# Sixteen-row blocks by DMA for the base inverse of a gated delta-rule kernel, and a new order of the turn

## The reference

```python
xn = layernorm(x)
# attention: q, k, v = silu(conv4(xn @ W)); k *= 128 ** -0.5
# alpha, beta = sigmoid(xn @ Wa + ba), sigmoid(xn @ Wb + bb)
def step(S, inps):                      # one token; S is 128 x 128 for each batch and head
    qt, kt, vt, at, bt = inps
    err = S @ kt - vt
    S = at * S - bt * outer(err, kt)
    return S, S @ qt
S0 = zeros; o = scan(step, S0, tokens)
o = (o - mean(o)) * rsqrt(var(o) + 1e-5) * ln_w + ln_b
attn = (o * sigmoid(xn @ Wg)) @ Wo
# experts: 512 tokens, 16 experts, top 4, silu(gate) * up, down, weighted sum
out = x + attn + moe
```

## Time and profile before

| | us |
|---|---|
| median of three runs | 3923.6 |
| the profiled execution | 3925.09 |
| its span, first to last instruction | 3923.5 |
| PE busy | 3769.9 (96%) |
| DVE, ACT, POOL busy | 2704.0, 2204.4, 1281.8 |
| mean granted TensorE clock | 0.986 |
| `prepare` ends on PE | 476.1 |
| `heads`, first to last instruction on DVE and POOL | about 486 to 3549.4 |
| `project` ends | about 3918 |

### The profile page before, as it was taken

How to read it: one execution, slowest core, us unless ns; L and a number is a source line. 1 busy time by engine, 2 the same in 40 slices (tenths; PEclk the granted TensorE clock), 3 DMA queues, 4 the chain that set the end, 5 groups by cost and what they waited for, 6 DMA issues and landing times. The chain is left out here.

```text
span 3923.5 us, 119759 instructions
## 1 busy us (share of the span) xinstructions
PE 3769.9 (96%) x41088; PEld 3063.9 (78%) x41088; DVE 2704.0 (69%) x6942; ACT 2204.4 (56%) x6016; POOL 1281.8 (33%) x2594
## 2 busy tenths in 40 slices
PE   7999889999999999999999999999999999987999
PEld 5777668888888888888788888888888888866887
DVE  3444458878788777788777778777887878863222
ACT  3433356666666666666666666666666666652111
POOL 3434433333333333333333333333333333320000
PEclk9999989999999999999999999999999999988999
DMA  3343341111111211111321111111111211215443
GB/s 134 111 147 141 117 128 45 51 45 47 45 45 48 55 50 46 45 48 48 90 88 46 45 48 48 45 48 45 47 49 45 48 45 45 50 24 163 144 146 109
DMA packets 371786, 275.67 MB, mean 70 GB/s; under 512 B 153457, under 2 KB 284529, under 8 KB 369361
## 3 DMA queue, kind: packets, MB, share of 16 engines
q1 hardware_dynamic: 368848, 261.29, 23.5%
q0 software_dynamic: 2560, 8.39, 0.6%
HBM read 209.85 MB, written 59.77 MB: 69 GB/s over the span
## 5 line engine op out<-in xcount | busy, mean ns | idle before, releaser
L1084 DVE SCALAR_TENSOR_TENSOR conv<-bank,tap,conv 128x512 f32<-128x512 f32 x1152 | 857.6, 744 | 79.3 <-ACT conv L1233 56.4
L1295 PE MATMUL bank<-hx_hi,w_hi 128*128 128x512 f32 x2048 | 874.2, 427 | 35.2 <-POOL w_lo L913 24.0
L1295 PE MATMUL bank<-hx_hi,w_lo 128*128 128x512 f32 x2048 | 899.4, 439 | 0.0
L1295 PE MATMUL bank<-hx_lo,w_hi 128*128 128x512 f32 x2048 | 881.5, 430 | 0.0
L1295 PEld LDWEIGHTS bank<-hx_hi,w_hi 128*128 128x128 f32 x2048 | 391.3, 191 | 71.7 <-issue 49.0
L1295 PEld LDWEIGHTS bank<-hx_lo,w_hi 128*128 128x128 f32 x2048 | 389.0, 190 | 50.7
L931 POOL TENSOR_TENSOR prods<-Lb,Tc 128x28 f32<-128x28 f32 (+6 forms) x896 | 203.6, 227 | 683.6 <-ACT Lb L1219 621.2
L1295 PEld LDWEIGHTS bank<-hx_hi,w_lo 128*128 128x128 f32 x2048 | 389.9, 190 | 40.1
L965 POOL TENSOR_TENSOR oG<-oT,gT 128x512 f32<-128x512 f32 x128 | 163.7, 1279 | 721.7 <-ACT oT L1254 721.7
L1037 DVE SCALAR_TENSOR_TENSOR S<-S,gamma,bank 128x128 f32<-128x128 f32 x480 | 163.6, 341 | 203.9 <-PE bank L1376 191.7
L1207 ACT ACTIVATE Wc<-bank 128x128 f32<-128x128 f32 x512 | 141.4, 276 | 242.4 <-PE bank L1367 242.3
(11 more groups left out here) (156 smaller groups left out, 8836.3 us busy)
## 6 DMA issues: line engine op xcount, KB each, us to landing
gamma<-gamma_d SPq DMA_DIRECT2D x128, 258.0 KB, 3.4
alpha<-alpha_d SPq DMA_DIRECT2D x128, 256.0 KB, 3.1
oT_d<-oG SPq DMA_DIRECT2D x128, 256.0 KB, 2.4
o_raw<-oT_d SPq DMA_DIRECT2D x32, 1024.0 KB, 6.8
gu_raw<-in_gate_up SPq DMA_DIRECT2D x17, 1408.0 KB, 6.3
dn_raw<-in_down SPq DMA_DIRECT2D x17, 512.0 KB, 4.5
x_in<-in_x SPq DMA_DIRECT2D x8, 1024.0 KB, 9.3
w_raw<-in_Wk SPq DMA_DIRECT2D x32, 256.0 KB, 3.6
```

The costliest lines, as they stand in the source:

```text
L1084: dve.scalar_tensor_tensor(out=conv[i][:, to], in0=PJ[PJ_OF[(g + 3) % 4][i]][:], scalar=tap[:, i, j + 1:j + 2], in1=conv[i][:, to], op0=AL ...
L1295: last = pe.matmul(dst, a[:, i, k], b[:, k, cols], start=(j == 0), stop=(j == 3 * KC - 1))
```

## The change

The base block of the inverse becomes 16x16 (`SB` 16, `LEVELS` gone), one merge level falls away, and the blocks of L get to GpSimd by DMA:

- VectorE's diag, Lc and Lx, TensorE's product with `same` and ScalarE's copy to `Lb` are gone. SyncE's new `spread` stores the eight 16x16 diagonal blocks of LT to DRAM, one DMA for each block, and reads them back with four loads, each of which names two blocks 16 times over, so that each of 32 partitions gets its block's 256 values of 4 chunks (4096 B).
- GpSimd's substitution has 15 steps of two instructions instead of 7. It waits for all four loads. The pipeline is one group deeper: group g+4 is projected, and its solve begins in slot 35 and ends in slot 13 of the next turn.
- TensorE has two visits a turn (slots 20 and 1) with three groups in each: 16 matmuls of 32x32, 8 of 32x32 and 4 of 64x64. `MT32` and the columns of `w32` keep the two merges apart.
- Products with the zero state are left out: the first chunk of a head has no S by kT and no q_gamma by S, the last no k_rows by Wc and one transpose less.
- The slots of nearly all operations are new; kT and gT have 6 buffers, qT, vT, decay and TT three; the loop over the heads is unrolled by 3; weights are cut in other slots; ScalarE cuts the first weights before it waits for constants.

```diff
-SB = 8
+SB = 16
 TB = 32
-LEVELS = [8, 16]
+NB = P // SB
 STEPS = 38
-CHAIN = {0: 0, 5: 1, 8: 2, 11: 3, 13: 4, 17: 5, 20: 6, 24: 7, 26: 8, 29: 9, 32: 10, 34: 11}
+UNROLL = 3
+CHAIN = {0: 0, 6: 1, 8: 2, 13: 3, 15: 4, 17: 5, 19: 6, 21: 7, 23: 8, 29: 9, 31: 10, 35: 11}
-A_AT, KT_AT, VT_AT, ON_TURN_AT, L_AT, BASE_AT = 1, 2, 11, 18, 24, 30
-VISIT_AT = {9: 0, 15: 1, 28: 2, 34: 3}
-SOLVE_AT = {34: (0, 2), 36: (2, 4), 0: (4, 6), 2: (6, 7)}
+A_AT, KT_AT, VT_AT, ON_TURN_AT, L_AT = 5, 0, 9, 26, 18
+VISIT_AT = {20: 0, 1: 1}
+SOLVE_AT = {35: (0, 1), 0: (1, 4), 3: (4, 6), 6: (6, 9), 7: (9, 11), 9: (11, 14), 13: (14, 15)}
+T16P_AT, POW_AT, QG_AT, OG_AT = 19, 12, 21, 23
+AT_AT, K_AT, T16_AT, TN64_AT, DECAY_AT, LT_AT = 4, 3, 17, 16, 7, 18
+CUT_AT = {(3, 22): 0, (3, 27): 1, (3, 30): 2, (0, 2): 3}
...
+        base_d = nc.dram_tensor("base_d", (2, P // SB, SB, G, SB), F32, kind="Internal").ap()
...
-        diag = sb("diag", [P, G, TB])
-        Lc = sb("Lc", [P, G, SB])
-        Lx = sb("Lx", [P, G, SB, SB])
-        Lb = sb("Lb", [P, G, SB, SB])
+        Lb = sb("Lb", [P, SB, G, SB])
...
+            def spread(hh, g, d):
+                at = counter(hh, g)
+                place = base_d[(g + d) % 2]
+                for q in range(NB):
+                    rows = slice(q * SB, (q + 1) * SB)
+                    if q == 0:
+                        sp.wait_ge(lt_done, at(1, d + 1))
+                    if q == NB - 1:
+                        wait(sp, solve_done, at(SOLVE_PER, d))
+                    sp.dma_start(place[q], LT[rows, (g + d) % 4, :, rows], allow_slow_non_contiguous=True)\
+                      .then_inc(base_stored[q // 2], 16)
+                for i in range(NB // 2):
+                    sp.wait_ge(base_stored[i], at(32, d + 1))
+                    sp.dma_start(Lb[i * TB:(i + 1) * TB].rearrange("p i c t -> p (i c t)"),
+                                 place[2 * i:2 * i + 2].rearrange("b (o i) c t -> b o (i c t)", o=1)
+                                 .to_broadcast([2, SB, SB * G * SB])).then_inc(base_loaded[i], 16)
...
                             if i == 0:
-                                pool.wait_ge(lb_done, at(1, d + 1))
+                                for loaded in base_loaded:
+                                    pool.wait_ge(loaded, at(16, d + 1))
                             wait(pool, solve_done, at(SOLVE_PER, d, k))
-                            pool.tensor_tensor(prods[:, :, i + 1:], Lb[:, :, i + 1:, i],
+                            pool.tensor_tensor(prods[:, :, i + 1:], Lb[:, i, :, i + 1:],
                                                Tc[:, :, i:i + 1].to_broadcast([P, G, SB - 1 - i]), ALU.mult)\
                                 .then_inc(solve_done, 1)
...
-                    if inv and s == T8P_AT:
-                        pool.wait_ge(solve_done, at(SOLVE_PER, 3))
+                    if inv and s == T16P_AT:
+                        pool.wait_ge(solve_done, at(SOLVE_PER, 4))
...
+                    if inv and s == T16_AT:
+                        dve.wait_ge(t16_done, at(1, 4))
+                        wait(dve, mid_done, at(2, 1, 1))
+                        wait(dve, tn_placed, at(2, 2))
+                        dve.transpose(Tnb[:, par], TTb[:, par]).then_inc(tn_done, 1)
...
                     if proj and s == LT_AT:
-                        dve.wait_ge(l_done, at(1, 4))
+                        dve.wait_ge(l_done, at(1, 5))
...
-                    if proj and s == DIAG_AT:
-                        (wait; 4 x tensor_tensor into diag; tensor_reduce into Lc)
-                    if proj and s == LX_AT:
-                        (wait; tensor_tensor into Lx)
...
+                    if r == 0 and not first:
                         pe.wait_ge(s_done, at(4, 0, c + 1))
...
+                        if not first:
+                            pe.matmul(w[:, 3 * D:], q_gamma[:, cur, chunk(c)], S[:], start=True, stop=False)
+                        last = pe.matmul(w[:, 3 * D:], AT[:, cur, c], Wc[:], start=first, stop=True)
+                        if not final:
+                            last = pe.matmul(w[:, 2 * D:3 * D], k_rows[:, cur, c], Wc[:], start=True, stop=True)
...
-                    if proj and s == BASE_AT:
-                        pe.wait_ge(lx_done, at(1, 4))
-                        pe.matmul(TR[:, 0:G * SB * SB], same[:], Lx[:].rearrange("p c t i -> p (c t i)"),
-                                  start=True, stop=True).then_inc(spread_done, 1)
```

560 lines of the change are left out of this document (273 added, 287 removed).

## The result

The changed kernel takes 5074.6 us (median of 4 runs, 5069.4 to 5076.4) against 3925.4 before (3923.4 to 3930.1): a ratio of 1.292, 95% interval 1.291 to 1.294. The prediction was 4682 with a range up to 4980. The direction and the mechanism were right, the size was 393 us short. The profiled execution took 5076.4, its span is 5074.8.

The account below looks back on a forecast made before the run. TensorE bounds the kernel before, at 23.1 us a turn; after, a serial loop through DRAM and GpSimd: 16.0 + 10.05 + 1.0 + 0.6 + 0.4 + 0.75 = 28.8 us, times 127 plus the rest 4682 us, range 4430 to 4980.

Parts of the forecast that it names:

- The loop: LT, stores, loads, solve, TTb, transpose, next LT: a serial chain through DRAM and GpSimd, 28.8 us a turn.
- solve with hrstd, to TTb: GpSimd's 30 solve instructions, 10.05 us (bounds 9.6 to 10.6), plus 1.0 for hrstd before the last step.
- TTb, transpose, to LT: GpSimd's TTb 0.6 us, then VectorE's transpose and wake 0.4, ahead of the next LT.
- the stores' issue: SyncE's eight stores at 0.42 us each, so the first load is issued at 3.5 us (bounds 2.8 to 4.1).
- The landing: Lb loads after the first issue: 2.1 us plus 10.4 for the bytes on two engines, complete at 16.0.
- The number of engines: DMA engines sharing an Lb load: two, from its outermost count of 2; chance 0.80.
- The range: Whole kernel's time: 4430 to 4980 us around 4682, from low and high bounds of the loop's terms.
- The rival with 16 engines: Lb loads use 16 engines, Lb complete at 8.2 us, loop 21.0, time 3683 us; chance 0.16.
- Its rule: Lb complete below 10.1 us after LT makes the kernel faster than before, above it slower.
- TensorE alone: TensorE's own work without the loop: 23.1 - 0.9 - 1.18 - 0.2 = 20.8 us a turn.
- The loop not closed: Rival: LT needn't wait for VectorE's transpose, two turns share the path, 25 us a turn, about 4190; chance 0.01.
- The granted clock: TensorE's clock falling in the new idle time: cost left out of the sum, TensorE having 8 us a turn to spare.

Follow-up runs that it names:

- The shared stores: Changed kernel with the stores of blocks 0 to 3 issued from ScalarE's queue, the others from SyncE's and loaded first: 4768.7 us.
- the two sizes: Changed kernel with 512 KB of Lb loads, 5074.6 us, and the same with four loads at half their bytes, 256 KB, 4430.6 us.
- The eight loads: Changed kernel with eight loads of one block, each named 16 times, instead of four loads of two blocks: 4160.5 us.
- without the loop: Changed kernel without the stores of LT's blocks and the loads of Lb, GpSimd solving from constant zero: 3717.5 us.
- in slot 21: Changed kernel with eight one-block loads, all stores on SyncE, hrstd behind TTb, visit in slot 23, copies in 25, transpose in 21: 4099.5 us.
- two slots of one transpose: Kernel with eight loads, SyncE stores, hrstd behind TTb, visit in 23, copies in 25: transpose moved from slot 21 to 19, 3845.1 us against 4099.5.
- the wide pieces: Changed kernel with each store moving 16 full rows of LT, pieces of 2048 B, instead of 64 pieces of 64 B: 4898.6 us.
- the one with eight loads: Changed kernel with eight one-block loads, transpose behind LT, and stores of blocks 0 to 3 issued from ScalarE's queue: 3943.2 us.
- half the bytes: Changed kernel with four two-block loads of eight rows each, the rest of Lb zero: 4430.6 us.

## Why the prediction was right in kind and short in size

The loop, term by term, as predicted and as the means of 127 turns of the trace have it:

| term | predicted | measured | x 127 turns |
|---|---|---|---|
| end of LT to the first load's issue | 3.5 | 5.83 | +296 |
| from there to the solve | 12.5 | 13.57 | +136 |
| solve with hrstd, to TTb | 11.19 | 10.89 | -38 |
| TTb, transpose, to LT | 0.86 | 0.95 | +11 |
| LT | 0.75 | 0.69 | -8 |
| sum | 28.8 | 31.9 | +397 |

The third row is that of the 97 turns without a low part of weights in the solve; in the other 30 it is 12.15, which makes 38 us against the 40 predicted. 4684 + 397 - 2 is 5079, against 5076.4. Nothing outside the loop was off by more than a few us: the first LT was done at 507.1 and not 510, and from the last LT's end to the kernel's end are 476 us where 474 were predicted.

- **The step that failed is the stores' issue:** "I take 0.42 each: the first load is issued at 3.5 (bounds 2.8 to 4.1)". Eight stores take 5.7 us, 0.71 each on the mean, and the first load is issued at 5.8, beyond the upper bound. The bounds came from gamma and scale, whose issues keep their price in the changed kernel (0.34 and 0.39). Two rows of another shape were treated as if they bounded every issue. The shared stores confirm the term: with the first load at 3.4 the time is 4769, inside the predicted range.
- **The landing was 1.0 short.** Its rate was right (10.4 predicted, 10.4 by the two sizes); the part that does not depend on bytes is 3.1, not the 2.1 of beta's row. The packets of the trace split the 13.5 another way (medians of turns 40 to 109): 1.4 from the first load's issue to its first packet, 11.4 in which Lb's 128 packets of 4096 B go two at a time, and 0.7 to the solve. The median packet takes 0.16 us, which alone would make 10.2; why the mean is 0.18 stayed open.
- **The number of engines,** on which 0.80 of the chance lay, was right: 51 GB/s at a share of 0.13, and 13.5 that become 5.9 with 16 as the outermost count.
- **The range** had all its high bounds together at 31.5 us and 5020, which is a wrong sum: 4.1 + 2.1 + 12.2 + 10.6 + 2.75 is 31.75, and the time 5060. It was then cut to 4980 because both ends together were unlikely. The measured loop of 31.9 lies above even the right sum, since the bound of one term was no bound.
- **The rival with 16 engines** was priced at 3683, with Lb complete at 8.2. The eight loads make this case nearly: the solve starts at 11.9 and the time is 4160.5, still slower than before. 2.4 of the 3.7 us between are the same wrong price of a store's issue; the rest goes with the issues of twice as many loads, which the rival left out. Its rule held: 1.8 us above 10.1, times 127, on top of 3925 is 4154. The chance of 0.17 for faster was too high for that reason.
- **TensorE alone** was put at 20.8 from a turn of 23.1, so 2.3 less. By medians a turn goes from 23.2 to 21.2 without the loop, 2.0 less, and by means from 23.4 to 21.6, 1.8 less. That was hidden under the loop, and no run splits it over the product with `same`, the visits and the zero-state products.
- **The loop not closed** (4190): putting the transpose behind LT makes this case; 4549, as the wrong price of the stores and of the landing is in its loop too, and in TensorE's part of it the lower clock.
- **The granted clock** fell to 0.83 from 0.99 in the loop's idle time, as left out of the sum. In the changed kernel it costs nothing that shows: none of TensorE's work lies in the loop, and TensorE is idle for 8.6 us a turn (818 of 3080 us). It does cost where TensorE's slots are part of the loop or nearly fill the turn, as with the transpose behind LT and in slot 21.

## What to carry to other kernels

When the instruction that starts the next trip through DRAM stands behind the one that ends the last, the trip is a serial loop, and every instruction that issues it counts in full. Bytes that nobody waits for were free here (80 instead of 54 GB/s cost nothing). Price the issues from rows of the same shape, or give them a wide bound (here a store's issue was 1.7 times the price taken from the nearest rows), and look at the outermost count of a broadcast load before anything else: the same 512 KB took 13.5 us with 2 there and 5.9 with 16. When such a loop is shortened until it fits, what is left is queue order: the copy or transpose for which TensorE waits must not stand behind other work, and two slots of one transpose were worth 250 us.

## What the runs showed of the hardware

- A store of 64 pieces of 64 B takes SyncE 0.64 us from start to start at the median, and one of 16 pieces of 2048 B takes 0.46, while the issues of gamma and scale last 0.34 and 0.39. In 81 of 128 turns of the changed kernel one of the eight stores' issues lasts about 1.3 us instead of 0.59, which makes the mean 0.71 (0.55 with the wide pieces). Shared over two queues, four stores took 3.2 us on either in the kernel with two-block loads, and 2.5 on SyncE and 2.7 on ScalarE in the one with eight loads (medians). What sets this price beyond the pieces, and what the long issues are, is open.
- A load on two engines delays what is issued behind it on the same queue: oT_d, 0.3 us behind the last load, lands after 10.3 us instead of 2.4, and gamma after 9.1 (3.4 on the page of before); with eight loads gamma lands in 3.8, with half the bytes oT_d in 5.5. alpha, issued when the loads are done, keeps its 3.3. In the 3.7 us looked at above, what is left of oT_d moves between Lb's packets, two packets at a time in all.
- Four stores issued by ScalarE occupy it for 2.7 us, in which it copies nothing.
